# Scores of two heads at once: 64 rows of the array for each, in the attentions with 512 keys

## What is computed

```
scores = einsum("bhqd,bhkd->bhqk", q, k) * scale      # 256 queries x 512 keys, contraction over 16
scores = where(mask, scores, -inf or the lowest float)
attn   = softmax(scores)
out    = einsum("bhqk,bhkd->bhqd", attn, v)            # then a projection, and the residual
```

## Time and profile before

| | |
|---|---|
| median of 3 runs (lowest to highest) | 1101.68 us (1100.23 to 1102.01) |
| the profiled execution: its own time, its span | 1103.04 us, 1101.2 us |
| mean granted TensorE clock | 0.936 of full speed |
| busy over the span: TensorE, its weight loads, VectorE, ScalarE, GpSimd | 87%, 73%, 71%, 55%, 28% |
| L2a, 862 to 942 us of the span, busy: the same five | 71.5, 50.6, 65.9, 63.7, 43.4 of 80 us |
| L3a, 975 to 1055 us of the span, busy: the same five | 71.0, 49.4, 64.8, 63.1, 43.4 of 80 us |

### The profile page before, as it was taken

How to read it: one execution, slowest core, us unless ns; L and a number is a source line. 1 busy time by engine, 2 the same in 40 slices (tenths; PEclk the granted TensorE clock), 3 DMA queues, 4 the chain that set the end, 5 groups by cost and what they waited for, 6 DMA issues and landing times. The chain is left out here.

```text
span 1101.2 us, 17924 instructions
## 1 busy us (share of the span) xinstructions
PE 954.1 (87%) x6616; PEld 808.7 (73%) x6616; DVE 782.7 (71%) x1627; ACT 604.4 (55%) x1369; POOL 312.4 (28%) x321
## 2 busy tenths in 40 slices
PE   4889886779999999997889999998678799779958
PEld 4666665667988889887778898888557566566647
DVE  3486766367787878787578787787594688567864
ACT  3587873134555555553355565555353688277851
POOL 3454540040112222221102222110003456344520
PEclk8899997878999999999799999999978899789989
DMA  4995006130001111110001111000023930294020
GB/s 140 271 231 87 1 1 237 28 138 1 34 7 39 39 40 39 39 37 22 20 1 39 40 39 39 1 1 1 21 99 99 240 62 1 83 242 72 5 83 20
DMA packets 39490, 72.71 MB, mean 66 GB/s; under 512 B 6534, under 2 KB 23944, under 8 KB 37228
## 3 DMA queue, kind: packets, MB, share of 16 engines
q1 hardware_dynamic: 39404, 71.56, 24.2%
HBM read 55.28 MB, written 16.27 MB: 65 GB/s over the span
## 5 line engine op out<-in xcount | busy, mean ns | idle before, releaser
L1308 ACT CAST L1a_probsT_hi<-L1a_bank 128x512 fp32r<-128x512 f32 x128 | 68.8, 589 | 94.2 <-PE L1a_bank L1189 94.2
L1147 POOL TENSOR_SCALAR L1a_wo_hi<-L1a_stage 128x512 fp32r<-128x512 f32 x16 | 10.7, 670 | 362.5 <-PE L1a_sums L74 356.1
L1425 DVE TENSOR_REDUCE L1a_top<-L1a_scores 128x2 f32<-128x1024 f32 x64 | 78.2, 1222 | 36.1 <-PE L1a_scores L74 36.1
L1340 ACT ACTIVATE L1a_probs<-L1a_scores,L1a_neg_max 128x512 f32<-128x512 f32 x128 | 86.9, 684 | 30.2 <-DVE L1a_bias_shifted L1429 25.2
L1363 DVE TENSOR_TENSOR L1a_probsT_lo<-L1a_bank,L1a_probsT_hi 128x512 fp32r<-128x512 f32 x128 | 82.0, 682 | 0.1
L72 PE MATMUL L1a_bank<-L1a_probsT_hi,L1a_v_hi 128*128 128x256 f32 x256 | 73.1, 286 | 9.2 <-DVE L1a_probsT_lo L1363 9.2
L1310 ACT ACTIVATE L1a_attended_hi<-L1a_bank,L1a_cols 128x256 fp32r<-128x256 f32 x64 | 30.5, 476 | 90.4 <-PE L1a_bank L74 90.4
L72 PE MATMUL L1a_bank<-L1a_w_hi,ctxT_hi 128*128 128x256 f32 x256 | 76.6, 299 | 0.0
L73 PE MATMUL L1a_bank<-L1a_w_lo,ctxT_hi 128*128 128x256 f32 x256 | 73.8, 288 | 0.0
L417 POOL TENSOR_SCALAR L0a_probs<-L0a_probs,L0a_inverse 128x768 f32<-128x768 f32 x64 | 57.2, 906 | 58.7 <-DVE L0a_inverse L686 58.7
L74 PE MATMUL L1a_bank<-L1a_w_hi,ctxT_lo 128*128 128x256 f32 x256 | 73.8, 288 | 0.0
(11 more groups left out here) (410 smaller groups left out, 3106.3 us busy)
## 6 DMA issues: line engine op xcount, KB each, us to landing
L1a_stage<-in_L_w SPq DMA_DIRECT2D x15, 1024.0 KB, 4.8
L0m_fold_wq<-in_L_wqT SPq DMA_DIRECT2D x2, 2048.0 KB, 13.0
L0a_k_dram<-L0a_kT_hi SPq DMA_DIRECT2D x8, 384.0 KB, 10.6
L0a_k_stack<-L0a_k_dram SPq DMA_DIRECT2D x4, 576.0 KB
L0a_w_qkv<-L0a_k_dram SPq DMA_DIRECT2D x4, 576.0 KB
L0a_wide_wo<-in_L_wo SPq DMA_DIRECT2D x1, 2048.0 KB, 16.6
L0a_wide_wo<-in_L_wo SPq DMA_DIRECT2D x2, 1024.0 KB, 17.7
L0m_stage<-in_L_wm SPq DMA_DIRECT2D x4, 512.0 KB, 6.5
```

Of the source, the lines that this page charges most:

```text
L1308: nc.scalar.copy(out, source).then_inc(ring.hi_done, 1)
L1340: nc.scalar.activation(probs[:, g % 2, qt, :], scores[:, qt, :], ACT.Exp, bias=neg_max[:, g % 2, qt:qt + 1], accum_out=row_sum[:, g % 2, q ...
L1425: link(nc.vector.tensor_reduce(top[:, :], scores[:, :, :], AX.X, ALU.max))
```

## The change

For 512 keys (`beside`), one step takes one query tile of both heads of a pair. `q_stack` has one copy, with the even head's rows in 0 to 47 and the odd head's in 64 to 111, over a background of ones. A step issues two matmuls, one on rows 0 to 63 and one on rows 64 to 127 of the array, into two banks, after one wait. So the tiles come in another order: m = 2g + a is head 2(g // 2) + a, query tile g % 2, and both tiles of a head are complete after two steps. `made(m)` gives head and query tile of tile m, `nth` is its inverse. Transposes and the product of v still go head by head; their wait and the slot that they read follow from `nth`. There are 12 slots for probabilities and small values in place of 8. GpSimd sets the background of `q_stack` with one memset. In L2a two steps of each batch, not one, compute `spoiled`. L0a keeps its form.

```diff
--- before.py
+++ after.py
@@ -227,11 +227,14 @@
 
         k_stack = [ph.sb("k_stack", [P, 4, nk], F32R),
                    w_qkv[:, :, :, :].rearrange("p s i n -> p (s i n)")[:, 0:4 * nk].rearrange("p (t n) -> p t n", t=4)]
-        q_stack = [ph.sb(f"q_stack{i}", [P, 2, 4, Q], F32R) for i in range(2)]
-
-        score_slots, probs_slots, small_slots = (4, 8, 8) if nk == S else (2, 6, 8)
+
+
+        beside = nk == S
+        q_stack = [ph.sb(f"q_stack{i}", [P, 1 if beside else 2, 4, Q], F32R) for i in range(2)]
+
+        score_slots, probs_slots, small_slots = (4, 12, 12) if beside else (2, 6, 8)
         probs = ph.sb("probs", [P, probs_slots, nk])
-        spoiled = ph.sb("spoiled", [P, 2])
+        spoiled = ph.sb("spoiled", [P, 2, 2])
         TSLOTS = 5
         probsT = ph.sb("probsT", [P, TSLOTS, 2 * nkt * P])
 
@@ -314,6 +317,12 @@
                     order.append(("B", 0, 0))
             order += [("T", t, c) for c in range(tj)]
         order.append(("V", units - 1, 0))
+
+        def made(m):
+
+            return (m // 4 * 2 + m % 2, m // 2 % 2) if beside else (m // 2, m % 2)
+
+        nth = {made(m): m for m in range(2 * HEADS)}
 
         def slot_scores(m):
             return scores[:, m % score_slots, 0:nk]
@@ -361,7 +370,7 @@
                 if o == 1:
                     for other in range(1, OCTETS):
                         write(other)
-                sp.wait_ge(cleared[r], 3)
+                sp.wait_ge(cleared[r], 2 if beside else 3)
                 if o == 0:
                     sp.wait_ge(mask_written, 16)
                 if o >= 2:
@@ -374,7 +383,7 @@
                 for a in range(2):
                     rows = slice(64 * a, 64 * a + 48)
                     sp.dma_start(raw(k_stack[r][rows, :, :]), k_dram[o, a:8:2, :, :, :].rearrange("t r c n -> (r c) t n")).then_inc(stack_loaded[r], 16)
-                    sp.dma_start(raw(q_stack[r][rows, a, :, :]), q_dram[o, a:8:2, :, :, :].rearrange("t r c n -> (r c) t n")).then_inc(stack_loaded[r], 16)
+                    sp.dma_start(raw(q_stack[r][rows, 0 if beside else a, :, :]), q_dram[o, a:8:2, :, :, :].rearrange("t r c n -> (r c) t n")).then_inc(stack_loaded[r], 16)
                 if o == 1 and cfg["bias_values"]:
                     for other in range(2, OCTETS):
                         sp.wait_ge(written[other], 96)
@@ -403,11 +412,14 @@
                     nc.gpsimd.memset(padding, 0.0).then_inc(padding_set, 1)
                     if cfg["bias_values"]:
                         nc.gpsimd.memset(spread[:, :, :, :], 0.0).then_inc(spread_clear, 1)
-                nc.gpsimd.memset(raw(q_stack[r][:, :, :, :]), 0.0).then_inc(zeroed, 1)
-                pool.wait_ge(zeroed, r + 1)
-                for a in range(2):
-                    nc.gpsimd.memset(raw(q_stack[r][64 * a + 32:64 * a + 64, a, :, :]), 1.0).then_inc(cleared[r], 1)
-                pool.wait_ge(cleared[r], 2)
+                if beside:
+                    nc.gpsimd.memset(raw(q_stack[r][:, :, :, :]), 1.0).then_inc(cleared[r], 1)
+                else:
+                    nc.gpsimd.memset(raw(q_stack[r][:, :, :, :]), 0.0).then_inc(zeroed, 1)
+                    pool.wait_ge(zeroed, r + 1)
+                    for a in range(2):
+                        nc.gpsimd.memset(raw(q_stack[r][64 * a + 32:64 * a + 64, a, :, :]), 1.0).then_inc(cleared[r], 1)
+                    pool.wait_ge(cleared[r], 2)
                 if r:
                     pool.wait_ge(ring.full, u0)
                 nc.gpsimd.memset(raw(k_stack[r][:, :, :]), 0.0).then_inc(cleared[r], 1)
@@ -465,14 +477,14 @@
                 last.then_inc(ring.full, 1)
 
             def transpose_head(g):
-                pe.wait_ge(normed, 2 * g + 2)
+                pe.wait_ge(normed, max(nth[g, 0], nth[g, 1]) + 1)
                 for c in range(tj):
                     job = job_of["T", g, c]
                     ring.wait_bank(pe, job)
                     for i in range(4):
                         qt, kt = divmod(4 * c + i, nkt)
                         last = nc.tensor.transpose(ring.bank(job)[:, i * P:(i + 1) * P],
-                                                   probs[:, (2 * g + qt) % probs_slots, kt * P:(kt + 1) * P], keep["ident"][:, :])
+                                                   probs[:, nth[g, qt] % probs_slots, kt * P:(kt + 1) * P], keep["ident"][:, :])
                     last.then_inc(ring.full, 1)
 
             def product_v(unit):
@@ -497,14 +509,22 @@
                     r = octet % 2
                     if e == 0:
                         pe.wait_ge(stack_loaded[r], 16 * stack_dmas * (octet // 2 + 1))
-                    for qt in range(2):
-                        m = 2 * g + qt
-                        if m >= score_slots:
-                            pe.wait_ge(exp_done, m - score_slots + 1)
-                        for c0, n in [(0, S)] + ([(S, extra)] if extra else []):
-                            last = nc.tensor.matmul(slot_scores(m)[:, c0:c0 + n], q_stack[r][:, e % 2, e // 2, qt * P:(qt + 1) * P],
-                                                    k_stack[r][:, e // 2, c0:c0 + n], start=True, stop=True)
-                        last.then_inc(scores_full, 1)
+                    if beside:
+                        if 2 * g + 1 >= score_slots:
+                            pe.wait_ge(exp_done, 2 * g + 2 - score_slots)
+                        for a in range(2):
+                            half, qt = np.s_[64 * a:64 * a + 64], g % 2
+                            nc.tensor.matmul(slot_scores(2 * g + a), q_stack[r][half, 0, e // 2, qt * P:(qt + 1) * P],
+                                             k_stack[r][half, e // 2, :], start=True, stop=True).then_inc(scores_full, 1)
+                    else:
+                        for qt in range(2):
+                            m = 2 * g + qt
+                            if m >= score_slots:
+                                pe.wait_ge(exp_done, m - score_slots + 1)
+                            for c0, n in ((0, S), (S, extra)):
+                                last = nc.tensor.matmul(slot_scores(m)[:, c0:c0 + n], q_stack[r][:, e % 2, e // 2, qt * P:(qt + 1) * P],
+                                                        k_stack[r][:, e // 2, c0:c0 + n], start=True, stop=True)
+                            last.then_inc(scores_full, 1)
                 if t >= 0:
                     if product_before(t) is not None:
                         product_v(product_before(t))
@@ -601,7 +621,7 @@
                         small = m % small_slots
                         act.wait_ge(max_done, m + 1)
                         if m >= probs_slots:
-                            act.wait_ge(ring.full, job_of["T", (m - probs_slots) // 2, tj - 1] + 1)
+                            act.wait_ge(ring.full, job_of["T", made(m - probs_slots)[0], tj - 1] + 1)
                         nc.scalar.activation(probs[:, m % probs_slots, :], slot_scores(m), ACT.Exp,
                                              bias=neg_max[:, small:small + 1],
                                              accum_out=row_sum[:, small:small + 1]).then_inc(exp_done, 1)
@@ -677,12 +697,13 @@
                     if 2 * g - 2 >= small_slots:
                         dve.wait_ge(normed, 2 * g - small_slots)
                     sums = row_sum[:, small:small + 2]
-                    if cfg["nan_if_masked"] and (g - 1) % H == 0:
-
-
-                        link(nc.vector.tensor_scalar(spoiled[:, :], neg_max[:, small:small + 2], -MASKED, 0.0, ALU.mult, ALU.mult))
-                        link(nc.vector.tensor_tensor(spoiled[:, :], spoiled[:, :], sums, ALU.add))
-                        sums = spoiled[:, :]
+                    if cfg["nan_if_masked"] and (g - 1) % H < (2 if beside else 1):
+
+
+                        own = spoiled[:, (g - 1) % 2, :]
+                        link(nc.vector.tensor_scalar(own, neg_max[:, small:small + 2], -MASKED, 0.0, ALU.mult, ALU.mult))
+                        link(nc.vector.tensor_tensor(own, own, sums, ALU.add))
+                        sums = own
                     nc.vector.reciprocal(inverse[:, small:small + 2], sums).then_inc(inverse_done, 1)
                 if t >= 0:
                     if product_before(t) is not None:
```

## The result

| | before | after |
|---|---|---|
| median (lowest to highest), 7 runs each on one chip | 1102.01 us (1100.23 to 1106.34) | 1110.94 us (1107.04 to 1114.48) |
| ratio of the times, 95% interval | | 1.0071 [1.0054, 1.0089] |
| the profiled execution: its own time, its span | 1103.04, 1101.2 | 1113.34, 1111.5 |
| mean granted TensorE clock | 0.936 | 0.932 |

The kernel became slower by 0.7%, outside the range given. The medians differ by 8.9 us; the spans of the two profiled executions differ by 10.3 us, since the one after was itself 2.4 us above its median. I cut both spans at starts of instructions on VectorE: the first maximum of a loop, each low part of the product of v, and the first statistics of L3a, where its front begins. The end of L2a's loop, from its seventh low part to these statistics, takes 12.3 or 12.4 us in both and is left out.

What follows compares the result with a forecast made beforehand. Pace was taken as set by VectorE's own work and one hand-over with ScalarE; terms 0 + 2.4 + 0.3 + 0.4 - 2.2 + 0, plus 0.2 for loop ends, gave +1.1: 1102.8 us, range 1099.5 to 1108.8.

Steps and rivals of the forecast that it cites:

- Term 1: Score matmuls, from head 12's transposes to step 18's maxima: 0 us; shape changes cost c (0.25) each, within slack 1.0.
- rival D: The two score matmuls do not run beside each other, nothing of 0.25 is saved: 1103 to 1106 us, chance 0.05.
- Rival B: Changes of shape, c above 0.37 each, set the pace in the steady loops: 6.0 us more, 1108.8, chance 0.18.
- Term 2: Even heads' transposes in both loops wait for a later tile, VectorE's copy 0.2 late, 12 times: +2.4 us.
- the ends of the loops: End of each loop, where the late head 28 stands before two products of v: 0.2 us added to the sum.
- term 5: Start of L3a: shorter TensorE wait for octet 1's DMA, so the clock stays up: -2.2 us.
- rival A: L3a's clock falls all the same at its start, so nothing is gained there: 1105.0 us, chance 0.18.
- Term 3: Start of L2a: later tiles and `spoiled` delay the fill by 1.5, step 8's DMA wait covers all but +0.3 us.
- Term 4: The second `spoiled` of L2a's second batch, in VectorE's full loop: +0.4 us.
- Term 6: Memsets, slots and semaphores, including a VectorE cast beside a memset in L3a's front: 0 us, bounds -0.9 and +0.2.

Runs made afterwards that it cites:

- k3_wait: Kernel before, with the transposes of an even head waiting for one scaled tile more (512 keys): 1105.05 us, ratio 1.0017 to before.
- r_after: The changed kernel itself, unaltered, measured and profiled once more: 1107.90 us, ratio 1.0045 to before.
- k1_lag4: Changed kernel, with transposes four steps behind the scores instead of three (LAG 4, 512 keys): 1106.49 us, ratio 1.0035 to before.
- k4_hold: Changed kernel, with GpSimd's memsets of L3a held until VectorE's last low part of the weights: 1107.75 us, ratio 1.0036 to before.
- k2_order: Changed kernel's order, slots and waits, but score matmuls on 128 rows, two copies of q and the old memsets: 1106.48 us, ratio 1.0026 to before.
- k7_order_lag4_hold: k2_order with LAG 4 and the memsets of L3a held: 1103.78 us, ratio 1.0009 to before.
- k5_before_hold: Kernel before, with the memsets of L3a held until VectorE's splits are over: 1100.90 us, ratio 0.9974 to before.
- k6_lag4_hold: Changed kernel with LAG 4 and the memsets of L3a held: 1102.85 us, ratio 0.9996 to before.

## Why the prediction was wrong, step by step

- **Term 1, score matmuls, 0: right.** Two of them take 0.50 in place of 0.72, so they run beside each other (not rival D). Scores to transposes is 882.93 - 882.51 = 0.42, where a pair that overlaps fully should take 0.25; transposes to scores is 1.03 in place of 0.85. By these estimates a change of shape costs 0.17 to 0.18, taken as 0.25 in the prediction, and the step without a wait is 1.45 in place of 1.35. Rival B needed c above 0.37 and VectorE waiting for scores; there is no such wait, and with LAG 4 the cycle is 9.12. The stretch of term 1 holds five changes and not four (two around each of the scores of steps 16 and 17, one ahead of those of step 18, counting the product of v as a change back), so the bound was 0.30; 0.18 lies under that too. The Trainium skill, TensorEngine Tiling (Array Packing), section Tiling Modes, has changes of mode emptying the engine: the trace agrees in direction, at 0.17.
- **Term 2, +2.4: right in mechanism and size for what it held.** 0.22 a cycle; k3_wait gives it with one tile more in the wait. Six cycles a loop hold 5 x 0.22 + 0.38 = 1.5, 3.0 in both with what the prediction had under the ends of the loops.
- **The step that failed is in term 2:** "VectorE's copy of these transposes started at 896.32: 0.2 late." It priced the wait by VectorE's delay. TensorE's own idle time ahead of these transposes went from 0.15 or less (0.54 at head 16) to 1.33, and to 2.13 where two `spoiled` stand ahead. The bound of 0.5 a head had no clock in it. I had read the clock only at the one long wait of L3a (term 5, rival A), and asked nowhere whether the new waits would make it fall. They did, three times: 5.4 us of the profile, 4.1 in r_after's. LAG 4 takes wait and falls away (k1_lag4).
- **Term 3, +0.3: too low.** Measured 1.0; the clock rises one head later. The cover of step 8's DMA was counted, the low level before it was not. In k4_hold, the same program up to here, head 1's transposes take 1.51 and not 1.97, and the start takes 18.96 and not 19.49.
- **Term 4, +0.4: right** for the instructions (904.74 to 905.13 and 907.00 to 907.39 on VectorE), but they also lengthen head 16's wait to 2.13, and the fall there costs 2.8 and not 1.3.
- **Term 5, -2.2: right in size**, -2.6 measured, and rival A did not come. The wait is 0.63, not the 1.7 forecast, as the slow clock lengthened this fill too. The reason given, "Less than L2a's 2.31, so the clock stays up", is no rule: in k2_order the clock fell there after 0.57, in k7_order_lag4_hold after 2.07, and in k5_before_hold it held after 2.82. It held in all five profiles with 64 rows and the late wait, but why is not shown, and to that extent the term was luck.
- **Term 6, 0 with bounds -0.9 and +0.2: wrong in sign.** The short memset ended early, but the cast did not follow it; it stood behind the next one, and the second cast behind the third. The casts became 1.7 longer and the front 1.9. k4_hold takes this away. Why the first cast let two memsets pass here and only one before is not shown. Before, a semaphore wait stood between the first memset and the next (955.90 to 955.95), and after, none does between `q_stack` and `k_stack`. But such a gap is not needed: between `k_stack` and `v`, and between `v` and the next `q_stack` (965.75), none stands either, and there the casts got through. Another difference is how long a cast had been held: the first one only 0.26 when the short memset ended, 2.0 when it got through, and the second 1.1. But the second cast of before had been held 0.24 and got through, with a gap. None of this was tried alone.
- **Sum.** By the terms +1.1; what was missed is 5.4 for falls, 1.9 for the front, 0.7 for the start of L2a, together 8.0, and 0.4 + 0.9 lie ahead of the first loop and behind the last; these make 10.4, against 10.3 between the spans. The 0.4 and 0.9 are no more than executions of one program differ by there (3.3 and 1.1 between the two profiles of after). Each of the two causes alone, undone, leaves 1.0035 and 1.0036; both undone leave 0.9996. Neither of the two was measured beside the kernel after itself, which stood at 1.0071 and at 1.0045, so the medians don't fix well what each cause is worth by itself.

What stays open: what decides whether the clock falls in a late wait; whether 64 rows by themselves make falls likelier; where the 2 us between k6_lag4_hold and k5_before_hold come from; and why after was 8.9 us slower in one measurement and 5.1 in the other. The number of falls explains 1.3 between the two profiles.

## What to carry to other kernels

When a reordering makes an engine wait longer, price the wait twice: by who is late behind it, and by what the clock of TensorE does after it, in windows of the trace around every new wait and not only around the longest. Where a step turns cheaper, look at what it then runs into: here the memset behind a shorter one held VectorE's cast, and steps of a cycle of 8.70 met the DMA of L3a earlier, with the clock down. If tiles of a head are completed later, try a longer lag of the consumer with it: here one step more took the wait away.

## What the runs showed of the hardware that was not expected

- TensorE's clock fell from 2.4 to 1.2 GHz after idle times of 1.33 us (887.62), yet held after another 1.33 (898.24), and in a second execution of the same program it held at a place where it had fallen (L3a, head 16). At step 8 of L3a it held after 2.82 (k5_before_hold) and fell after 0.57 (k2_order, with 1.10 of idle time just before), 2.07, 3.51 and 3.79. So the length of one wait does not decide; what does is not shown.
- The fall shows in the durations of the instructions that follow: eight transposes 1.97 for 1.09, the product of v up to 3.64 for 1.93.
- A step with two score matmuls on 64 rows each and eight transposes took 1.45 us, with matmuls on 128 rows 1.35. By estimate a change between 64 and 128 rows costs 0.17 to 0.18, there and back 0.35, and the overlap of the two matmuls saves 0.25.
- A cast of 128x512 from float32 took 0.42 to 0.43 with GpSimd still, 1.38 and 1.39 when it ended behind the memset that it had started beside, and 2.28 when it ended behind the next one. All four casts beside memsets ended 0.27 to 0.29 after one.
